# Four neighbouring tokens on a partition: a recurrent layer and a mixture of experts on one core

## The reference

```python
def reference(...):
    x = L0_attn_x3d                                  # (16, 256, 128) float32
    x = _layernorm(x + _L0_attn_ref(x, ...))
    x = _layernorm(x + _L0_ffn_ref(x, ...))
    return x

# attention stage: a linear recurrence over the 256 positions of a sequence
lam = exp(-exp(nu_log) + 1j * exp(theta_log));  gamma = sqrt(1 - abs(lam) ** 2)
Bu = einsum('bld,nd->bln', x3d, gamma[:, None] * (B_re + 1j * B_im))
states = scan(lam, Bu)                               # s[t] = lam * s[t-1] + Bu[t]
y = einsum('bln,mn->blm', states, C_re + 1j * C_im).real + x3d @ D_mat.T
out = x3d + sigmoid(res_logit) * (gelu(y @ W1) @ W2) # 128 -> 512 -> 128

# mixture of experts, over T = 4096 tokens, top 2 of 8 experts
probs = softmax(xf @ Wg);  weights, indices = top_k(probs, 2)
for e in range(8):
    h = gelu(xf @ W1[e] + b1[e]);  y = h @ W2[e] + b2[e]
    out = out + y * cw[:, e:e+1]                     # cw: 0 for experts not chosen
```

## Time and profile before

| | us |
|---|---|
| median of 3 runs | 424.04 |
| lowest and highest run | 421.11, 427.4 |
| span of the profiled execution, first to last instruction | 403.5 |

### The profile page before, as it was taken

One profiled execution on the slowest core, in us unless ns is written; L12 is line 12 of the kernel. 1 busy time (PEld: TensorE's weight loads), 2 busy tenths in 40 slices (PEclk: granted clock), 3 DMA queues, 4 the chain that ended last, 5 costly groups with the idle time before them and its releaser, 6 DMA issues.

```text
span 403.5 us, 6693 instructions
## 1 busy us (share of the span) xinstructions
PE 301.3 (75%) x1531; PEld 253.2 (63%) x1531; DVE 295.8 (73%) x787; ACT 259.8 (64%) x569; POOL 263.2 (65%) x297
## 2 busy tenths in 40 slices
PE   2368999869874788899993599999999999100440
PEld 1235777546653677799993599999999995000110
DVE  3998999998653799899995289999999995100160
ACT  3315688378563687899994389999999993000451
POOL 4793479508877010577787777877877777777560
PEclk9999999899996699899999599999999999855585
DMA  4736516700111210223321332333333361111772
GB/s 116 268 95 220 173 39 220 281 1 33 48 47 37 56 42 20 67 74 88 87 69 54 85 92 79 85 85 83 84 89 89 92 199 52 52 52 52 190 215 78
DMA packets 47627, 39.23 MB, mean 97 GB/s; under 512 B 5160, under 2 KB 40240, under 8 KB 47608
## 3 DMA queue, kind: packets, MB, share of 16 engines
q1 hardware_dynamic: 42104, 27.68, 23.9%
q0 software_dynamic: 5504, 11.35, 8.6%
HBM read 18.39 MB, written 20.62 MB: 97 GB/s over the span
## 4 chain that ended last, share of the span: by engine, by line
POOL 32%; PE 29%; DVE 13%; issue 13%; ACT 6%; DMA 5%; SPq 0%; DVEq 0%; ACTq 0%; POOLq 0%
POOL slots_d L431 17%; POOL results_d L437 13%; PE bank L1016 8%; PE bank L1018 7%; PE bank L1017 7%; PE bank L1102 2%; DVE work L688 1%; PE bank L1119 1%; ACT fw L611 1%; DMA late<-slots_d 1%; DMA slots_d<-rows,slot_i 1%; ACT h L515 1%; DVE wuse L878 1%; DVE work L682 1%; DMA logs<-in_L_attn_res_logit_dram 1%
## 5 line engine op out<-in xcount | busy, mean ns | idle before, releaser
L437 POOL DMA_INDIRECT results_d<-work,dest x108 | 119.2, 1103 | 33.0 <-issue 32.0
L431 POOL DMA_INDIRECT slots_d<-rows,slot_i x64 | 72.1, 1127 | 49.4 <-DVE rows L834 19.1
L569 ACT ACTIVATE h<-bank,buse 128x384 f32<-128x384 f32 x144 | 84.1, 584 | 7.1 <-PE bank L1018 3.7
L915 DVE TENSOR_TENSOR h_l<-h,h_h 128x384 fp32r<-128x384 f32 x144 | 80.0, 556 | 6.3 <-ACT h_h L574 3.3
L1016 PE MATMUL bank<-h_h,wuse 128*128 128x384 f32 (+1 forms) x176 | 70.6, 401 | 3.9 <-DVE h_l L915 2.4
L1017 PE MATMUL bank<-h_l,wuse 128*128 128x384 f32 (+1 forms) x176 | 62.0, 352 | 0.0
L1018 PE MATMUL bank<-h_h,wuse 128*128 128x384 f32 (+1 forms) x176 | 61.9, 352 | 0.0
L1016 PE MATMUL bank<-xt_h,wuse 128*128 128x384 f32 x144 | 50.6, 351 | 3.7 <-ACT h L569 2.4
L878 DVE CAST wuse<-fw 128x1024 fp32r x72 | 49.8, 692 | 0.8 <-issue 0.8
L1017 PE MATMUL bank<-xt_l,wuse 128*128 128x384 f32 x144 | 49.5, 344 | 0.0
L1018 PE MATMUL bank<-xt_h,wuse 128*128 128x384 f32 x144 | 49.5, 344 | 0.0
(11 more groups left out here) (204 smaller groups left out, 651.8 us busy)
## 6 DMA issues: line engine op xcount, KB each, us to landing
late<-slots_d SPq DMA_DIRECT2D x36, 195.0 KB
late<-in_L_ffn_W_dram SPq DMA_DIRECT2D x16, 256.0 KB, 2.8
slots_d<-zeros SPq DMA_DIRECT2D x3, 1300.0 KB, 7.8
slots_d<-zeros SPq DMA_DIRECT2D x3, 1040.0 KB, 6.8
work<-results_d SPq DMA_DIRECT2D x10, 256.0 KB, 5.5
work<-in_L_attn_x3d_dram SPq DMA_DIRECT2D x8, 256.0 KB, 3.4
out_dram<-fw SPq DMA_DIRECT2D x8, 256.0 KB, 3.1
results_d<-work,dest POOLq DMA_INDIRECT x108
```

What stands on the lines that cost most here:

```text
L431: pool.indirect_dma_start(out=slots_d, out_offset=bass.IndirectOffsetOnAxis(ap=slot_i[:, k, i:i + 1], axis=0), in_=rows[:, k, i, :], in_of ...
L437: pool.indirect_dma_start(out=results_d, out_offset=bass.IndirectOffsetOnAxis(ap=dest[:, SQ * g + q:SQ * g + q + 1], axis=0), in_=yo[:, g ...
L569: act.activation(h32[:, b % 2, 0:SLOTS], H_PS[b % 2][:, 0:SLOTS], ACT.Gelu, bias=buse[:, k, b:b + 1]).then_inc(sm["gelu_b"], 1)
L915: dve.tensor_tensor(ht_l[b], h32[:, b % 2, 0:SLOTS], ht_h[b].bitcast(F32), ALU.subtract).then_inc(sm["hbl_ready"], 1)
```

## The change

Token `512 c + 128 q + p` of chunk `c` lay on partition `p`, in tile `q`. Now token `512 c + 4 p + q` lies there, so a partition holds four neighbouring tokens, and x and the output move in runs of 2 KB on each partition instead of four runs of 512 B. The scratch `results_d` changes from "all first results, then all second" (row `k T + token`) to pairs (row `2 token + k`), so one transfer of 4 KB runs brings both results of a chunk, with one semaphore `y_loaded`.

The columns with features on partitions stay in the order of time. So ACT's two copies in `x_copy` now read the PSUM bank `XT_PS` with a step of 128 elements (512 bytes) between neighbours and write in order, and the stationary tile of PE in `logits` and `r_transposed` is every fourth column of `rt` (a step of 16 bytes). PE and DVE read the results at the end in four runs of 128 elements.

```diff
-    x_t = x.rearrange("b s d -> (b s) d").rearrange("(c q p) d -> c p q d", q=QT, p=P)
-    out_t = out.rearrange("b s d -> (b s) d").rearrange("(c q p) d -> c p q d", q=QT, p=P)
+    x_t = x.rearrange("b s d -> (b s) d").rearrange("(c p q) d -> c p q d", q=QT, p=P)
+    out_t = out.rearrange("b s d -> (b s) d").rearrange("(c p q) d -> c p q d", q=QT, p=P)
...
-            return place[:, 2 * at * CHUNK:2 * (at + 1) * CHUNK].rearrange("p (a n) -> p a n", a=2)
+            return place[:, 2 * at * CHUNK:2 * (at + 1) * CHUNK]
+
+        def y_of(c, k):
+
+            return y01(c).rearrange("p (q a d) -> p q a d", q=QT, a=2)[:, :, k, :]
...
-        y0_loaded = [sem(f"y0_loaded{i}") for i in range(NCH)]
-        y1_loaded = [sem(f"y1_loaded{i}") for i in range(NCH)]
+        y_loaded = [sem(f"y_loaded{i}") for i in range(NCH)]
...
-                src = results_d[0:2 * T, :].rearrange("(a c q p) d -> c a p q d", a=2, q=QT, p=P)[c]
-                for a in range(2):
-                    sp.dma_start(y01(c)[:, a].rearrange("p (q d) -> p q d", q=QT), src[a]).then_inc((y0_loaded, y1_loaded)[a][c], 16)
+                src = results_d[0:2 * T, :].rearrange("(c p r) d -> c p (r d)", r=2 * QT, p=P)[c]
+                sp.dma_start(y01(c), src).then_inc(y_loaded[c], 16)
...
-            pool.iota(tok[:], [[P, NT]], base=0, channel_multiplier=1, allow_small_or_imprecise_dtypes=True)
+            pool.iota(tok[:, :].rearrange("p (c q) -> p c q", q=QT), [[2 * P * QT, NCH], [2, QT]], base=0, channel_multiplier=2 * QT, allow_small_or_imprecise_dtypes=True)
...
+            def by_token(t, by_tile=False):
+
+                return t.rearrange("n (q p) -> n p q", q=QT) if by_tile else t.rearrange("n (p q) -> n p q", q=QT)
+
             def x_copy(c):
...
-                act.copy(xt32[:, c % 3, :], XT_PS[:])
+                act.copy(by_token(xt32[:, c % 3, :]), by_token(XT_PS[:], True))
                 wait(act, sm["y_ready"], c - 1)
-                act.copy(xt_h[:, c % 2, :], XT_PS[:]).then_inc(sm["xt_sb"], 1)
+                act.copy(by_token(xt_h[:, c % 2, :]), by_token(XT_PS[:], True)).then_inc(sm["xt_sb"], 1)
...
-                    dve.tensor_scalar(rows[:, k, t0:t0 + n, D], s12[:, k, 0:n], float(k * T - 2 * T - off), None, ALU.add)
+                    dve.tensor_scalar(rows[:, k, t0:t0 + n, D], s12[:, k, 0:n], float(k - 2 * T - off), None, ALU.add)
...
-                dve.wait_ge(y1_loaded[c], 16)
-                dve.tensor_tensor(r3[:, k].rearrange("p q d -> p (q d)"), SUM_PS[c % len(SUM_PS)][:], y01(c)[:, 1], ALU.add).then_inc(sm["f_r"], 1)
+                dve.wait_ge(y_loaded[c], 16)
+                dve.tensor_tensor(r3[:, k], SUM_PS[c % len(SUM_PS)][:, :].rearrange("p (q d) -> p q d", q=QT), y_of(c, 1), ALU.add).then_inc(sm["f_r"], 1)
...
+            def tile_of_r(q):
+
+                return rt[:, :].rearrange("n (p q) -> n q p", q=QT)[:, q, :]
...
-                    last = mm(LG_PS[:, q * E:(q + 1) * E], rt[:, q * P:(q + 1) * P], wgc[:], start=True, stop=True)
+                    last = mm(LG_PS[:, q * E:(q + 1) * E], tile_of_r(q), wgc[:], start=True, stop=True)
...
-                    last = pe.transpose(R_PS[:, q * D:(q + 1) * D], rt[:, q * P:(q + 1) * P], ident[:])
+                    last = pe.transpose(R_PS[:, q * D:(q + 1) * D], tile_of_r(q), ident[:])
...
-                pe.wait_ge(y0_loaded[c], 16)
-                mm(SUM_PS[c % len(SUM_PS)][:], ident[:], y01(c)[:, 0], start=False, stop=True).then_inc(sm["f_sum"], 1)
+                pe.wait_ge(y_loaded[c], 16)
+                mm(SUM_PS[c % len(SUM_PS)][:, :].rearrange("p (q d) -> p q d", q=QT), ident[:], y_of(c, 0), start=False, stop=True).then_inc(sm["f_sum"], 1)
```

## The result

The changed kernel took 428.46 us (median of 20 runs, 423.81 to 433.27), the kernel before 426.75 us on the same chip (20 runs, 421.11 to 430.27). The ratio of the two is 1.0076, 95% interval 1.0043 to 1.011: 0.8% or 3.2 us slower (1.8 to 4.7), where +2.65 us were forecast. The ratio leaves out the slow executions of either kernel (those over 1.5% above its fastest, of which the profiled one, with 433.02 us, is one), and the two medians by themselves lie only 1.7 us apart. By the forecast's bound of 2% that is no change. Two repetitions gave 1.0051 (1.0013 to 1.009) and 1.0034 (0.9997 to 1.0071).

A forecast was written before the change was run, and what follows sets the result against it. No engine bounds the whole: PE bounds the first stage from 34.3 to 62.1 us, POOL from 164.3 us, then a tail chain. Terms 1.7 + 0.4 + 0.3 + 0.45 - 0.2 = +2.65 us take 424.04 to 426.6 us; range 420 to 432.

The forecast's parts named there:

- PE's stepped loads: First stage: 24 loads from `rt` on the path, each 0.07 us more, +1.7 us; bounds nothing and 5.0 us.
- rival of 0.25 us a load: First stage: each of PE's 36 stepped loads costs 0.25 us more, 435 us in all; chance 10%.
- ACT's copies: First stage: ACT's two copies out of PSUM with a 512-byte step, +0.4 us; upper bound 0.8 for the pair.
- the last chunk's transposes: Mixed part before the second dispatch: four transposes at half clock, +0.3 us, between 0 and 1.1.
- The first load: Tail: PE waits for one 512 KB transfer of results, 3.5 us instead of 3.01, +0.45 us; bounds -0.3 and +0.9.
- goes through to the end undiminished: Tail: the first load's +0.45 us reaches the end in full, because what follows is not bound by loads.
- The last store: End of the tail: 256 KB after the last issue move faster, -0.2 us, between -0.4 and 0.
- The tail's 2.41 us: Tail: DVE's standstill before 385.43 us is PE's passes, not loads; the gap stays 2.4 us.
- if the gap in the tail closes: Sign against the forecast: DVE's gap before chunk 4, expected to stay 2.4 us, closes.
- the rival built on loads: Tail: the 2.41 us gap is chunk 4's second result load, so faster loads close it, 421.1 us; chance 17%.
- The rival of runs cut the same: DMA engines cut runs into the same small packets, rates stay 293 GB/s, sum +3.3 us, 427.3 us; chance 8%.
- that of congestion: DMA congestion at the start and around 70 us is on the path, hidden; 9 us or more earlier, 415 us; chance 3%.

The follow-up runs named there:

- step_on_dve: Changed kernel with DVE writing `rt` in tile order, 512 bytes apart, so PE reads in order; dispatch 1 starts at 165.70 us, no ratio given.
- after_third: The changed kernel again, unaltered, on a chip where the kernel before takes about 405 us; ratio to the kernel before 1.0034 (0.9997 to 1.0071).
- step_8_bytes: Kernel before with PE's loads from `rt` at a step of 8 bytes; product loads cost 4 ns more, no ratio given.
- x_out_only_2: Second run of the kernel before with only x and output in 2 KB runs, PE and ACT steps included, results in two transfers; ratio 0.9997.
- after: The changed kernel's first profiled execution, 433.02 us, from the runs with ratio 1.0076 to the kernel before.
- after_again: The changed kernel again, no edit, for a second profile; ratio to the kernel before 1.0051 (1.0013 to 1.009).
- step_loads_only: Kernel before with only PE's loads of `rt` (lines 1033 and 1039) at a step of 16 bytes; ratio 1.0013, +0.5 us.
- x_out_only: Kernel before with only x and output in 2 KB runs, PE and ACT steps included, results in two transfers a chunk; ratio 1.002, +0.9 us.

## Why the prediction was right, and where its steps were off

The forecast had the direction, and two of the four places that it named for a loss show one. The number was in part luck, as the terms below show. The prediction's 426.6 us should also read 426.7 (424.04 + 2.65).

**PE's stepped loads, forecast +1.7 us.** Right in kind and somewhat small. Over the six profiles in which PE reads with 16 bytes, dispatch 1 starts at 165.1 us on average (163.78 to 166.39); over seven in which it reads in order or with 8 bytes, at 163.1 (162.08 to 164.27; step_on_dve, where PE waits for DVE instead, is left out): +2.0 us, against the +2.4 us of all three terms ahead of that point. All of it is there at POOL's first dispatch already, 92.3 against 90.3 us on average over the same profiles, and there the two sets do not overlap (91.28 to 93.84 against 89.53 to 91.09). A load with its product costs (1.64 - 0.79) / 8 = 0.106 us more, not 0.07. The count was off too. The transposes, a third of the 24 loads, pay 0.03 us for four. In the kernel after a third group of products stands on the chain (65.67 us), where before's has gone over to ACT and DVE; PE is busy there in both, and a chunk of the changed kernel takes 11.4 us instead of 10.5. Two groups of each kind give 1.8 us and three 2.6. The chains of the five other profiles show no third, so how much of it counts is not shown. The rival of 0.25 us a load is excluded.

**ACT's copies, +0.4, and the last chunk's transposes, +0.3.** Both are nothing. The first one's upper bound came from DVE's reads of SBUF, and PSUM at 512 bytes cost 0 of its 0.41 us. The last transposes take 0.85 us on the chain before and after. At a granted clock of 0.50 their four loads take 230 ns each in either kernel, in order and with 16 bytes; and nothing is added between the first dispatch (+2.0 us) and dispatch 1 (+2.0 us). The term had been put at +0.3 without a row for such a load.

**The first load, +0.45 on 3.01.** Mis-sized: the seven profiles with one transfer of 512 KB have 3.50 to 3.99 us, 3.75 on average, the three with the old 256 KB 2.82 to 3.02, 2.95 on average. That is +0.8, near the upper bound; the five with runs of 4 KB alone have 3.67, +0.7. The two with 256 KB in 2 KB runs have 2.57 and 2.80, so long runs give 0.3 us and waiting for both halves takes 1.0. The rate was as assumed, shown by the windows at the end of the kernel after against the 292 and 293 of the earlier trace rows (last two columns: DMA share and GB/s):

```profile
408.00:410.00 2.00, 0.79 (x2) 0.49 (x3) 0.00 (x0) 2.00 (x6) 0.82 (x2) 1.00 1.01 410
410.00:412.00 2.00, 2.00 (x6) 0.86 (x5) 1.57 (x5) 0.59 (x2) 0.00 (x0) 1.00 1.01 375
```

The 2.8 us for the first 256 KB were right (2.69 measured); the next 256 KB took 1.0 us and not the 0.67 that 394 GB/s would give.

That this delay "goes through to the end undiminished" is not borne out. From the start of the last send-back to DVE's start on chunk 4 (line 965) the four profiles with one transfer on the chips with 405 us have 11.0 to 12.2 us, 11.8 on average, and the three with the old loads 11.1 to 11.8, 11.6 on average. So 0.8 us at the load is 0.2 us there. The spread of over 1 us comes from PE's clock, which the next term but one shows, and with so few profiles it isn't shown how much of the delay arrives.

**The last store, -0.2.** The shortest landing of a store is 2.2 us before and 2.0 after, and so are the medians of the stores issued from 390 us on (2.2 in before, 2.0 in after_third), as forecast.

**The tail's 2.41 us are PE's passes: held, but not their length.** The chain's end in two more profiles shows it. The first is after_third:

```profile
373.85 3.69 DMA work<-results_d
377.59 2.07 PE bank L1176 x2
379.66 1.92 PE bank L1168 x3
381.71 1.71 issue
383.42 0.70 DVE late L971
```

and step_8_bytes, whose loads of results are those of before:

```profile
373.30 3.02 DMA work<-results_d
376.36 2.08 PE bank L1166 x2
378.44 1.92 PE bank L1158 x3
380.49 1.67 issue
382.16 0.70 DVE late L965
```

The gap is 1.7 us here with either kind of load, and 2.41 in the earlier trace rows. In x_out_only_2, whose first load lands soonest, it is 2.49. What goes with it is the moment at which the granted clock leaves 0.50 (1.2 GHz), which it shows after PE has stood idle for 32 to 34 us. In after_third, whose first pass starts at 377.59 us, this is in the window

```profile
381.00:382.00 1.00, 1.00 (x3) 0.46 (x2) 0.68 (x6) 0.00 (x0) 0.21 (x2) 0.64 0.94 209
```

and in the kernel before, whose first pass starts at 378.90 us, only in this one:

```profile
384.00:385.00 1.00, 1.00 (x3) 0.52 (x2) 0.00 (x0) 0.28 (x1) 0.60 (x2) 0.77 1.21 289
```

In the execution called "after" PE had worked until the last send-backs, its clock was 1.00 (2.4 GHz), the first two passes took 1.13 us instead of 2.08, and the gap was 0.62 us. In after_again the first two took 1.12 us too, but then the clock fell to 0.50 (from 403 to 406 us), and the gap was 2.32 us. That the gap "stays 2.4 us" was thus wrong as a number. By the prediction's own words it is wrong "if the gap in the tail closes"; it did nearly close in "after", but through PE's clock and not through faster loads, so the rival built on loads falls.

**The sum.** +2.0 + 0.7 - 0.2 = +2.5 us by the profiles' points; the three timings of the change say +3.2, +2.2 and +1.4 us (each ratio by its before). The forecast of +2.65 was met by terms of which two were too small and two were nothing, and that they cancelled is luck. The points are losses at their own places and not shown to arrive at the end (below). The rival of runs cut the same fell, since the packets did, and that of congestion, since no run came out faster by anything near 9 us.

**What stays open.** By parts the timings do not add up to the points. PE's steps should make step_loads_only 2.0 us slower and x_out_only about 1.6; they measure +0.5, +0.9 and -0.1 us. Only the interval of x_out_only (up to +2.2 us) holds the expected value; those of step_loads_only (up to +1.9) and x_out_only_2 (up to +1.1) do not. Some of the 2 us may be given back while POOL works off its list. On the chips with 405 us the two profiles in which PE reads with 16 bytes start dispatch 1 on average 1.8 us later than the six in which it does not and DVE doesn't write with a step, but the last send-back only 0.6 us later (371.61 and 373.93 against 371.06 to 373.60). The sets overlap, so this is a hint and no more. One profile shows the giving back most clearly: from dispatch 1 to the last send-back after_third needs 206.6 us and the kernel before 209.3, since POOL's send-backs there take 1080 instead of 1103 ns each. But that execution was the second shortest of its kernel's twelve (403.43 us beside a median of 407.38), and x_out_only_2 needs 209.1, so it is not shown that the change does it.

## What to carry to other kernels

Making runs longer pays only where the end waits for the transfer: here 13,441 packets fewer and 375 to 410 instead of 293 GB/s bought nothing that could be measured. Merging two transfers can cost: the first of two of 256 KB landed 1.0 us sooner than one of 512 KB. When a layout change puts a step somewhere, choose who reads with it by measuring the engine and the memory: PSUM read by ACT took 512 bytes for nothing and 16 bytes too, while DVE's read of SBUF with 512 bytes went from 808 to 1220 ns, and PE's loads of products from SBUF went from 192 to 329 ns at 16 bytes and stayed at 196 at 8. A loss at one place of the chain, however clearly a profile shows it, is not yet a loss at the end: here 2.0 us at the first dispatch came out as +0.5, +0.9 and -0.1 us. Compare the time of a profiled execution with the timed runs before building on it: here a span 20 us away from them was another kind of execution, not overhead.

## What the runs showed of the hardware

**Two kinds of execution.** In all five profiles from the sets of runs with about 426 us, the kernel after's among them, ACT stands still between 175 and 250 us, for a releaser that the trace cannot name. The waits of ACT in that stretch (us in total, times, longest):

```profile
ACT h L575 <- issue: 28.8, 2, 22.2
ACT rt L562 <- remote: 18.9, 2, 14.8
ACT h L575 <- remote: 11.0, 3, 7.1
ACT work L591 <- remote: 6.5, 1, 6.5
```

PE and DVE stop with it, and only POOL goes on with its queue of indirect DMAs. The windows of that kernel (columns as in the earlier trace rows):

```profile
190.00:222.70 32.70, 3.89 (x12) 3.29 (x12) 1.54 (x3) 1.46 (x4) 24.77 (x27) 0.59 0.16 53
222.70:250.00 27.30, 3.95 (x11) 2.95 (x12) 2.50 (x5) 3.65 (x8) 13.83 (x15) 0.50 0.12 36
250.00:300.00 50.00, 49.87 (x283) 45.72 (x283) 44.49 (x115) 43.97 (x104) 29.64 (x27) 0.96 0.26 72
```

The same kernel on one of the other chips, in after_third:

```profile
190.00:222.70 32.70, 26.02 (x159) 24.96 (x157) 26.86 (x71) 25.69 (x62) 25.69 (x24) 0.98 0.24 72
222.70:250.00 27.30, 23.15 (x129) 22.64 (x130) 17.93 (x46) 19.15 (x45) 21.20 (x21) 0.84 0.33 91
250.00:300.00 50.00, 50.00 (x309) 48.48 (x309) 47.40 (x123) 48.00 (x114) 39.62 (x35) 1.00 0.30 84
```

PE, DVE and ACT do almost nothing for 60 us and catch up afterwards; then PE bounds the rest (100.82 of 103 us from 300 on) and POOL waits for ACT, where on the others POOL bounds it. The change has no part in it, since before's own medians differ by the same 20 to 22 us. What ACT waits for was not tried and stays open.

**POOL's pace is faster where the other engines stand still.** A send-back takes 0.96 us when the experts are done (the last fifteen before the tail of the kernel before, by its chain), and 1070 to 1108 ns on average over the 108 of a profile. The stall shows the same: from 195 to 240 us the kernel after's dispatches take 958 ns and its send-backs 964, the kernel before's, whose engines work, 1103 and 1022. So the lower means of the kernel after (1070 ns for send-backs, 1018 for dispatches, against 1103 and 1127) belong to its kind of execution, not to the change. A spread of 38 ns in 108 instructions is 4 us, more than everything that this change moves.
